# Clearing semaphores on five engines, and the order of the first batch in a Mamba stage

## The reference, cut to what matters

```python
xr = x @ W_in.T
xc, res = xr[..., :DI], xr[..., DI:]                # DI = 512
u = silu(causal_depthwise_conv4(xc) + b_conv)
x_dbl = einsum('bdl,ed->ble', u, W_xproj)           # -> dt (16), B (16), C (16)
delta = softplus(dt @ W_dt.T + b_dt)
dA = exp(delta * A);  dBu = delta * B * u
h = dA_t * h + dBu_t                                # scan over the 512 tokens
y = (sum_n h*C + u * D) * silu(res)
return y @ W_out.T
```

## Time and profile before

| | |
|---|---|
| Median of 3 runs | 5533.48 us (5529.11 to 5542.79) |
| Profiled execution, its own time | 5545.86 us |
| Its span | 5544.1 us |
| Mean granted TensorE clock | 0.853 |
| Busy: PE, DVE, ACT, POOL | 4205.1, 2846.9, 1767.7, 2062.7 us |
| Delta stage | 0 to 969 us |
| Tanh MLP, multi-query, expert choice | 975 to 1137, 1139 to 1884, 1886 to 2410 us |
| SiLU attention, SwiGLU | 2413 to 3139, 3143 to 3438 us |
| Mamba | 3439 to 4781 us (POOL's memset of `sel` starts it at 3439.49 and takes 3.51) |
| Top-2 mixture | 4783 to 5540 us |

### The profile page before, as it was taken

The page is one execution under the profiler, slowest core; times in us unless marked ns, Lnnn a source line. Parts: engine busy times, 40 slices in busy tenths (PEclk is TensorE's granted clock), DMA queues, the critical chain, the costliest instruction groups (busy, mean ns, idle before and its releaser), DMA issues. The chain is left out here.

```text
span 5544.1 us, 58698 instructions
## 1 busy us (share of the span) xinstructions
PE 4205.1 (76%) x20078; PEld 2539.2 (46%) x20078; DVE 2846.9 (51%) x4976; ACT 1767.7 (32%) x3177; POOL 2062.7 (37%) x2030
## 2 busy tenths in 40 slices
PE   4697797769999629827888697677777777599994
PEld 2575475436666429813444354222223222355662
DVE  4432642334444472335665222688888898621224
ACT  2212412323333202225555222444444444111222
POOL 3433033222222216531222112467766677440113
PEclk8777888889999859968999798777778878799997
DMA  4531341110000339843433201112122212260113
GB/s 115 189 109 43 87 144 33 56 47 8 16 8 8 106 112 296 245 148 93 125 104 97 65 31 36 57 60 65 56 62 63 65 61 67 85 203 22 46 46 137
DMA packets 325325, 473.15 MB, mean 85 GB/s; under 512 B 70999, under 2 KB 220823, under 8 KB 320903
## 3 DMA queue, kind: packets, MB, share of 16 engines
q1 hardware_dynamic: 309334, 439.06, 25.9%
q0 software_dynamic: 15696, 30.33, 2.0%
HBM read 343.65 MB, written 125.63 MB: 85 GB/s over the span
## 5 line engine op out<-in xcount | busy, mean ns | idle before, releaser
L2949 PE MATMUL mamba_pS<-mamba_hC,ident 128*128 128x512 f32 x1024 | 680.5, 763 | 287.9 <-POOL mamba_hC L3045 286.6
L3045 POOL TENSOR_TENSOR mamba_hC<-mamba_h_t,mamba_cb 128x512 f32<-128x512 f32 x512 | 666.1, 1304 | 363.0 <-DVE mamba_h_t L2667 350.7
L2667 DVE TENSOR_TENSOR_SCAN mamba_h_t<-mamba_pD,mamba_dB 128x512 f32<-128x512 f32 x512 | 623.0, 1217 | 62.4 <-ACT mamba_pD L2823 58.9
L2949 PEld LDWEIGHTS mamba_pS<-mamba_hC,ident 128*128 128x128 f32 x1024 | 209.9, 230 | 644.1 <-POOL mamba_hC L3045 558.8
L2823 ACT ACTIVATE mamba_pD<-mamba_delta,mamba_a_neg 128x512 f32<-128x512 f32 x512 | 345.6, 688 | 405.9 <-DVE mamba_h_t L2667 405.6
L2659 DVE TENSOR_TENSOR mamba_dB<-mamba_e_t,mamba_pB 128x512 f32<-128x512 f32 x512 | 340.9, 666 | 13.8 <-PE mamba_pB L2940 11.2
L2043 DVE TENSOR_REDUCE mha_nmax<-mha_pM 128x1 f32<-128x384 f32 (+3 forms) x352 | 216.9, 637 | 222.4 <-PE mha_pM L2325 220.1
L1676 POOL TENSOR_SCALAR mqa_prob<-mqa_prob,mqa_rinv 128x128 f32<-128x128 f32 (+3 forms) x256 | 137.7, 539 | 484.1 <-DVE mqa_rinv L1473 483.3
L1467 DVE TENSOR_REDUCE mqa_nmax<-mqa_pS 128x1 f32<-128x128 f32 (+3 forms) x256 | 124.6, 487 | 315.4 <-PE mqa_pS L1614 312.8
L1534 ACT ACTIVATE mqa_prob<-mqa_pS,mqa_nmax 128x128 f32<-128x128 f32 (+3 forms) x256 | 134.6, 526 | 459.0 <-DVE mqa_nmax L1467 459.0
L2162 ACT ACTIVATE mha_prob<-mha_pW 128x512 f32<-128x512 f32 (+1 forms) x352 | 190.4, 561 | 234.0 <-PE mha_pW L2343 232.4
(11 more groups left out here) (559 smaller groups left out, 9229.8 us busy)
## 6 DMA issues: line engine op xcount, KB each, us to landing
mamba_cb<-mamba_c SPq DMA_DIRECT2D x256, 256.0 KB, 3.0
expert_w<-in_L_ffn_W SPq DMA_DIRECT2D x48, 1024.0 KB, 5.8
delta_shared<-delta_w SPq DMA_DIRECT2D x64, 576.0 KB, 4.7
mha_qkT<-mha_parts_d SPq DMA_DIRECT2D x96, 256.0 KB, 6.5
delta_w<-delta_wst SPq DMA_DIRECT2D x32, 576.0 KB, 2.8
expert_w<-in_L_ffn_W SPq DMA_DIRECT2D x48, 256.0 KB, 6.4
top_w<-in_L_ffn_w SPq DMA_DIRECT2D x24, 512.0 KB, 10.3
top_xg<-top_slots SPq DMA_DIRECT2D x71, 128.5 KB, 2.0
```

What stands on the lines that cost most here:

```text
L2667: nc.vector.tensor_tensor_scan(h_t[:, n % RB, :], pD[n % 2][:, :], dB[:, n % RB, :], 0.0, ALU.mult, ALU.add).then_inc(z["scan_ready"], 1)
L2949: nc.tensor.matmul(pS[i][:, :], c.ident[:, :], hC[:, n % RB, :], start=(s == 0), stop=(s == NS - 1))\
L3045: nc.gpsimd.tensor_tensor(hC[:, n % RB, :], h_t[:, n % RB, :], cb[:, r % RC, :], ALU.mult)\
```

## The change

Three things. `Scope.clear` deals the semaphores out to five engines in turn: number i of the list is cleared by SP, ACT, DVE, PE or POOL as i mod 5 is 0, 1, 2, 3 or 4. In Mamba's batch 0 POOL builds `sel` behind `variance(1)` and a wait for both scalings; PE waits for it only ahead of `broadcast_b(0)`; the gate products and `gate_in` move behind the steps products and behind `log`, and `silu_z(0)` into the loop of batch 0, unit 24, directly ahead of `silu_z(1)`. And `square(0)` becomes one DVE operation over all four tiles. Batches 1 to 7 keep their order.

```diff
@@ Scope.clear
-        for s in self.sems:
-            self.nc.sync.sem_clear(s)
+        engines = (self.nc.sync, self.nc.scalar, self.nc.vector, self.nc.tensor, self.nc.gpsimd)
+        for i, s in enumerate(self.sems):
+            engines[i % len(engines)].sem_clear(s)
         self.nc.all_engine_barrier(sem_only=True)
@@ stage_mamba
-        T_AT, Z_AT, CONV_AT, XP_AT, DT_AT = 0, 2, 2 + CT, 2 + 2 * CT, 3 + 2 * CT
+        T_AT = 0
+
+        def z_at(a):
+            return 3 + 2 * CT if a == 0 else 2
+
+        def conv_at(a):
+            return 2 if a == 0 else 2 + CT
...
@@ vector
+                def square(a):
+                    dve.wait_ge(z["decay_ready"], a + 1)
+                    nc.vector.scalar_tensor_tensor(every(e_t[:, a % 2, :, :]), every(decay), -2.0, every(decay), ALU.add, ALU.mult)\
+                        .then_inc(z["quad_ready"], CT)
...
                 split_high(0)
                 split_low(0)
+                square(0)
                 upper(0)
@@ scalar
                 for ct in range(CT):
-                    gate_in(0, ct)
-                for ct in range(CT):
                     conv_in(0, ct)
-                silu_z(0)
                 silu_u(0)
...
                 log(0)
+                for ct in range(CT):
+                    gate_in(0, ct)
                 act.wait_ge(z["pz"], 5)
...
                                 if u == 24:
+                                    if a == 0:
+                                        silu_z(0)
                                     silu_z(a + 1)
@@ tensor
                 pe.wait_ge(z["w_in"], 16 * 10)
-                pe.wait_ge(z["pz"], 4)
                 for k in range(KD):
                     turn(0, k)
-                for ct in range(CT):
-                    gate(0, ct)
                 for ct in range(CT):
                     conv(0, ct)
...
                 for ct in range(CT):
                     steps(0, ct)
+                pe.wait_ge(z["pz"], 4)
                 broadcast_b(0)
                 broadcast_b(1)
+                for ct in range(CT):
+                    gate(0, ct)
@@ gpsimd
-                nc.gpsimd.memset(sel[:, :, :], 0.0).then_inc(z["pz"], 1)
...
                 variance(0)
                 variance(1)
+                pool.wait_ge(z["xn_done"], 2)
+                nc.gpsimd.memset(sel[:, :, :], 0.0).then_inc(z["pz"], 1)
+                pool.wait_ge(z["pz"], 1)
+                for i in range(3):
+                    part = sel[BC * i:BC * (i + 1), :, :]
+                    nc.gpsimd.affine_select(out=part, in_=part, compare_op=ALU.not_equal, fill=1.0,
+                                            base=0, pattern=[[-1, BC], [0, P]], channel_multiplier=1).then_inc(z["pz"], 1)
+
+                pool.wait_ge(z["pz"], 4)
                 pool.wait_ge(z["a_exp"], 1)
                 nc.gpsimd.tensor_scalar(every(a_neg), every(a_neg), -1.0, None, ALU.mult).then_inc(z["pz"], 1)
-                for ct in range(CT):
-                    square(0, ct)
```

More of the change, by code:

```diff
@@ L2566, in store_c @@
                 def store_c(a):
-                    consumed(sp, use(a, XP_AT))
+                    consumed(sp, use(a, xp_at(a)))
                     sp.dma_start(c_d[a], xdbl[NS:BC, :]).then_inc(z["c_st"], 16)
@@ L2622, in split_high @@
                 def split_high(a):
-                    consumed(dve, use(a, XP_AT))
+                    consumed(dve, use(a, xp_at(a)))
                     if a >= 2:
@@ L2645, in steps @@
                     for i in (CT - 2, CT - 1):
-                        consumed(dve, use(a, DT_AT + i))
+                        consumed(dve, use(a, dt_at(a) + i))
                     step = every(delta[:, a % 2, :, :])
@@ L2687, in conv @@
                 def conv(a, ct):
-                    i = use(a, CONV_AT + ct)
+                    i = use(a, conv_at(a) + ct)
                     dve.wait_ge(z["tap0"], CT * a + ct + 1)
@@ L2771, in silu_z @@
                     for i in (CT - 2, CT - 1):
-                        consumed(act, use(a, Z_AT + i))
+                        consumed(act, use(a, z_at(a) + i))
                     nc.scalar.activation(every(res[:, a % 3, :, :]), every(res[:, a % 3, :, :]), ACT.Silu)\
@@ L2782, in xproj_in @@
                 def xproj_in(a):
-                    act.wait_ge(z["x_ps"], use(a, XP_AT) + 1)
+                    act.wait_ge(z["x_ps"], use(a, xp_at(a)) + 1)
                     if a:
@@ L2786, in xproj_in @@
                         act.wait_ge(z["c_st"], 16 * a)
-                    nc.scalar.activation(xdbl[:, :], pX[use(a, XP_AT) % 2][0:X, :], ACT.Copy)\
-                        .then_inc(x_free[use(a, XP_AT) % 2], 1)
+                    nc.scalar.activation(xdbl[:, :], pX[use(a, xp_at(a)) % 2][0:X, :], ACT.Copy)\
+                        .then_inc(x_free[use(a, xp_at(a)) % 2], 1)
                 def step_in(a, ct):
-                    act.wait_ge(z["x_ps"], use(a, DT_AT + ct) + 1)
+                    act.wait_ge(z["x_ps"], use(a, dt_at(a) + ct) + 1)
                     if a >= 2:
@@ L2794, in step_in @@
                         act.wait_ge(z["e_ready"], CT * (a - 1))
-                    nc.scalar.activation(delta[:, a % 2, ct, :], pX[use(a, DT_AT + ct) % 2][:, :], ACT.Identity,
-                                         bias=b_dt[:, ct:ct + 1]).then_inc(x_free[use(a, DT_AT + ct) % 2], 1)
+                    nc.scalar.activation(delta[:, a % 2, ct, :], pX[use(a, dt_at(a) + ct) % 2][:, :], ACT.Identity,
+                                         bias=b_dt[:, ct:ct + 1]).then_inc(x_free[use(a, dt_at(a) + ct) % 2], 1)
                 def decay_abs(a):
                     for i in (CT - 2, CT - 1):
-                        consumed(act, use(a, DT_AT + i))
+                        consumed(act, use(a, dt_at(a) + i))
                     if a:
@@ L2898, in turn, with turned_in @@
                     last.then_inc(z["x_ps"], 1)
+                def turned_in(a):
+                    for k in range(KD):
+                        consumed(pe, use(a, T_AT + k))
                 def gate(a, ct):
-                    out = into(use(a, Z_AT + ct))
-                    if ct == 0:
-                        for k in range(KD):
-                            consumed(pe, use(a, T_AT + k))
+                    out = into(use(a, z_at(a) + ct))
+                    if ct == 0 and a:
+                        turned_in(a)
                     for k in range(KD):
@@ L2910, in conv @@
                 def conv(a, ct):
-                    out = into(use(a, CONV_AT + ct))
+                    out = into(use(a, conv_at(a) + ct))
+                    if ct == 0 and a == 0:
+                        turned_in(a)
                     for k in range(KD):
@@ L2917, in xproj @@
                 def xproj(a, half):
-                    out = pX[use(a, XP_AT) % 2]
+                    out = pX[use(a, xp_at(a)) % 2]
                     if half == 0:
-                        into(use(a, XP_AT))
+                        into(use(a, xp_at(a)))
                         pe.wait_ge(z["u_ready"], a + 1)
@@ L2928, in steps @@
                 def steps(a, ct):
-                    out = into(use(a, DT_AT + ct))
+                    out = into(use(a, dt_at(a) + ct))
                     if ct == 0:
-                        consumed(pe, use(a, XP_AT))
+                        consumed(pe, use(a, xp_at(a)))
                     nc.tensor.matmul(out[:, :], w_dt[BC:X, ct * P:(ct + 1) * P], xdbl[BC:X, :], start=True, stop=True)\
```

28 lines of the change are left out of this document (14 added, 14 removed).

## The result

| | before | after |
|---|---|---|
| Median of 8 runs, us | 5531.82 (5521.35 to 5568.44) | 5494.23 (5482.52 to 5513.18) |
| Ratio of the two | | 0.9909 (0.9886 to 0.9932) |
| Profiled execution: own time, span | 5545.86, 5544.1 | 5491.08, 5489.3 |
| Mean granted TensorE clock | 0.853 | 0.859 |

A forecast was written before the change was run, and what follows sets the result against it. It took stages as serial, bounded by SP's clears between barriers and waits in Mamba's head. Clears 17.0 and head 19.75 less 1.9 gave 34.8 us, so 5498.7 us from a 5533.48 median; range 5486 to 5513.

The forecast's parts named there:

- clears: Gaps between stages: dealing 498 clears to five engines, with PE the slowest, gains 17.0 us.
- head, to first scan: Mamba's head: earlier conv products and DVE's polynomial, less a late table load, gain 19.75 us.
- `silu_z(0)` in the loop: Mamba's batch 0, unit 24: 1.91 us more ACT work with nothing to hide it, cost 1.9 us.
- The upper bound of the gain, 23.5: Gaps between stages: gain in us if every engine clears as fast as SP.
- Rival 2: Gaps between stages: clears do not run side by side, leaving only 17.8 us of gain, 5515.7 us; chance 0.06.
- the row's 1.31 us: ACT in Mamba's head: price of a table load, taken from exp's end to ln's start, without extra drain.
- The 0.3 us for a fourth `gate_in` late at ACT: Mamba's head: at the low clock ACT loads the Exp table 1.4 us late, of which 1.1 is hidden.
- Rival 1: Mamba's head: the clock stays low throughout, head gains 9.8 us, time 5506.7 us; chance 0.10.
- Rival 4: Mamba's head: POOL's table is held up by the taps; at 30 us long, 5504.8 us; chance 0.03.
- The clock is the unknown of the head: Mamba's head: PE idles between conv products, so the clock's level puts the head's gain between 9.8 and 21.8 us.
- rival 3: Last stage: PE work loses clock; at 0.85 it costs 37 us and the gain is gone, 5535; chance 0.04.

The follow-up runs named there:

- e2: Kernel before with only the clears dealt to five engines, Mamba's head as before; ratio to before 0.9970 (0.9945 to 0.9995).
- e3: Kernel after with all clears back on SP, so only Mamba's edits remain; ratio to before 0.9951 (0.9923 to 0.9980).
- e7: Kernel after with `silu_z(0)` left out; 5539.86 us in one execution.
- e12: Kernel after with the polynomial of batch 0 given back to POOL in eight operations; 5476.15 us in one execution.
- e17: Kernel after with all clears on SP and ACT alone clearing its 20 a second time in the first group; 5544.94 us in one execution.
- e5: Kernel after with PE clearing 6 semaphores once more just ahead of Mamba; 5565.48 us in one execution.
- e6: Kernel after with PE clearing 14 semaphores once more just ahead of Mamba; 5540.42 us in one execution.
- e9: Kernel after with five engines in the first clear only and SP in the other eight; 5472.11 us in one execution.
- e10: Kernel after with SP alone in the first clear and five engines in the other eight; 5546.49 us in one execution.
- e11: Kernel after with all clears on SP, the other four engines clearing theirs once more in the first clear; 5530.58 us in one execution.
- e4: Kernel after, unchanged, measured again; ratio to before 0.9910 (0.9880 to 0.9941).
- e16: Kernel after, unchanged, a third time; ratio to before 0.9896 (0.9846 to 0.9946).
- e8: Kernel after with SP clearing each run of consecutive semaphore numbers in one instruction; ratio to before 0.9899 (0.9877 to 0.9920).

## What held of the prediction, and the step that failed

| term | forecast | measured | read from |
|---|---|---|---|
| clears | 17.0 | 17.0 | gaps of before and after; 16.9 in e2 |
| head, to first scan | 19.75 | 20.7 | 81.6 to 60.9; 20.5 in e3 |
| `silu_z(0)` in the loop | -1.9 | -0.6 | e7's batch 0 |
| Mamba's later batches | 0 | 7.7 | loop 1259.6 to 1252.5 is 7.1, and the 0.6 above |
| delta stage, table loads | 0 | open | batch 2 comes 12.7 earlier (56.2 to 43.5), but this lead is gone halfway through the stage |

**The clears** were right for the reason given: PE decides, at 0.119 to 0.122 us a clear where 0.125 was taken from three neighbouring semaphore instructions. (The upper bound of the gain, 23.5, should read 23.8 by its own terms, 30.0 less 6.2; nothing hangs on it.) Rival 2 (engines not side by side) is refuted by the five rows of line 59.

**The head** was right step by step. Turns 11.5 us into the stage (11.7 forecast), on the last parameter DMA; first tap 18.7 (19.0); last tap 28.5 (28.8); the table load of `silu_u` 0.1 us behind that and `silu_u` itself 1.29 us behind the load's start, so the row's 1.31 us held and there is no second 1.3 us of drain; exp's end 47.5 (48.2); delta 10.2 us later (10.15), and e12 prices that part alone at 6.9 (6.95); first scan 60.9 (61.8). The 0.3 us for a fourth `gate_in` late at ACT did not occur after: the load began 0.1 us behind delta. Rival 1 (low clock throughout) did not come, but its mechanism exists: with this head the first scan came at 60.9 to 64.6 us, latest in e17, where the low level lay on the projection and the steps products. The trace of after is at the good end of that. Rival 4 (the table in the way) did not: it ended 3448.99, before the projection had.

**`silu_z(0)`** cost 1.8 us at its unit, as forecast, but the loop has slack behind it that the prediction denied from the one wait of the earlier trace rows: two thirds came back within the batch.

**The step that failed** is the first: "one layer follows the other, nothing overlaps, so a microsecond taken from a gap between two stages or from the head of one comes off the total unless a later stage gives it back". It counted only what the edited instructions themselves save and let every other stretch stand as it was, but for a loss. The runs showed that Mamba's later batches do not stand: put at nothing, they became 7.7 us shorter, nearly all in batches 2 to 5, where PE's clock rises earlier (the windows of batch 3; in e5 and e6 the same code has the old length). With the head and `silu_z(0)` a little better than priced, the terms add to 44.8 us in place of 34.8, which lies in the measured 50 (38 to 63). A second stretch moved too: the delta stage's load of batch 2, right behind the first clear, came 13 us earlier (e9, e10 and e11 put that on the other engines' instructions in that clear). What that is worth at the stage's end is not shown, so it is not in the sum; with the 12.2 us that the two traces differ there the terms would come near the 54.8 between them, but by a lead that was lost and another that was won by the clock. "The clock is the unknown of the head" looked for the clock in the head alone, and rival 3 put it in the last stage, which did not move (756.5 against 757 us, granted 0.90 both times).

There is luck in two places. The median came within 4.5 us of the forecast one although the forecast gain was short by 10 us of the terms and 15 of the ratio: the two medians lie closer together than the ratio says. And the short loop, which all three runs of the changed kernel had (after, e4, e16), is not the work's own: with the same Mamba code seven other runs had the long one, and there Mamba gained 17 to 19 us in place of 27.8.

Open: why the other engines' instructions in the first clear quicken the loads behind it and which of them count, what that is worth in the whole time, and why the clock rises earlier or later in Mamba's head behind the same gap.

## What to carry to other kernels

Price an edit from the nearest rows and follow it release by release; here that gave each local term within 1.3 us. Then treat every DMA-bound stretch behind an edit and every loop in which PE's clock changes level as able to move by 10 us either way, and read the same stretches, stage by stage, in a run of each part alone before crediting the edit, and follow a lead to the end of its stage before counting it. If many semaphores must be cleared between two barriers, clear runs of consecutive numbers in one instruction, rather than dealing them out: the gaps here fell to 3.8 us in place of 15.2, though the whole time did not show it.

## What the runs showed of the hardware

- A clear of a range costs far less than its single clears: in e8 26 semaphores took 68 ns, 57 took 122 and 98 took 195, where 98 single clears on SP take 5.6 to 6.1 us.
- PE is the slowest engine at clears in a row, 119 ns each in the trace of after, and SP the fastest, 59.
- The same Mamba code ran for 1313.4 us at a granted 0.82 and for 1322.8 at 0.80 (after and e5, which starts it 0.73 us later). Which of the two came went with the time from PE's first turn to the rise of its clock, 5.7 to 6.3 us or 7.9 to 8.8.
- Extra instructions on ACT, DVE, PE and POOL during the first clear, with no data of their own, shortened the 16 loads behind it: 27.9 us of SP's queue in e11 against 38.4 before, and batch 2 after 40.9 us in place of 49 to 57.
- The same 376 products of the delta stage took 36.6 us at a granted 0.79 and 46.4 at 0.56 (before and after).
